# Two gated expert networks on one core: banks, silu buffers and background pieces dealt anew

## What is computed

```python
# first expert network: E=8 experts, hidden 256, two experts kept for each token
w = top2_softmax(xf @ Wg + bg)
for e in range(E):
    h = gelu(xf @ W1[e] + b1[e])
    out += w[:, e:e+1] * (h @ W2[e] + b2[e])
# windowed attention over the last 16 tokens
g = sigmoid(tanh(x @ Wp.T + bp) @ Wg.T)
out = windowed_sum(g * x, 16) / windowed_sum(g, 16)
# second expert network: E=16 experts, hidden 128, two kept
hidden = silu(x @ w1[e]) * (x @ w2[e])
out += dispatch[:, e] * (hidden @ w3[e])
# each of the three reads a layer-normalised t and adds to it: t = t + stage(ln(t))
```

## Time and profile before

| | us |
|---|---|
| median of 3 runs | 502.32 (501.47 to 503.74) |
| the profiled execution | 500.19 |
| its span, first to last instruction | 498.2 |
| first network, about | 284 to 372 |
| second network, about | 372 to 498 |

### The profile page before, as it was taken

The page is one execution under the profiler, slowest core; times in us unless marked ns, Lnnn a source line. Parts: engine busy times, 40 slices in busy tenths (PEclk is TensorE's granted clock), DMA queues, the critical chain, the costliest instruction groups (busy, mean ns, idle before and its releaser), DMA issues.

```text
span 498.2 us, 8873 instructions
## 1 busy us (share of the span) xinstructions
PE 442.7 (89%) x2982; PEld 299.8 (60%) x2982; DVE 352.8 (71%) x1029; ACT 278.7 (56%) x667; POOL 156.2 (31%) x189
## 2 busy tenths in 40 slices
PE   2998999959978999899999989998888888979994
PEld 2687777734537899799999834443434444534452
DVE  3288779338875768788969754655567999777863
ACT  1477666632307898788889666655564244333431
POOL 4400000001230748185204332323251453433342
PEclk9999999988988999999999999998999999999998
DMA  8200000000030033000000022111011122131230
GB/s 192 121 2 1 2 1 0 1 1 1 0 84 1 3 85 87 1 1 3 1 2 1 2 87 87 47 62 43 22 67 64 44 88 64 36 108 62 72 117 16
DMA packets 13324, 20.91 MB, mean 42 GB/s; under 512 B 4480, under 2 KB 6144, under 8 KB 12768
## 3 DMA queue, kind: packets, MB, share of 16 engines
q1 hardware_dynamic: 13136, 20.25, 14.2%
q10 hardware_dynamic: 144, 0.11, 0.1%
HBM read 19.62 MB, written 0.72 MB: 41 GB/s over the span
## 4 chain that ended last, share of the span: by engine, by line
PE 54%; DVE 29%; issue 7%; ACT 5%; POOL 2%; DMA 1%; DVEq 0%; POOLq 0%; SPq 0%; ACTq 0%
PE PS L1771 9%; PE PS L1515 7%; PE PS L1531 6%; PE PS L1782 5%; PE PS L1695 4%; PE PS L1707 3%; DVE stage L1393 3%; PE PS L1793 2%; DVE M L1039 2%; PE PS L1476 2%; PE PS L1607 2%; DVE pr L1284 2%; PE PS L1620 2%; ACT score_arena L776 2%; PE PS L1723 2%
## 5 line engine op out<-in xcount | busy, mean ns | idle before, releaser
L1771 PE MATMUL PS<-YTs,WH 64*128 64x512 f32 x192 | 80.3, 438 | 5.8 <-DVE stage L1393 3.1
L573 POOL TENSOR_TENSOR pr<-pr 128x512 f32<-128x512 f32 x39 | 50.3, 1291 | 97.3 <-DVE pr L1284 65.0
L1771 PE MATMUL PS<-YX,WH 64*128 64x512 f32 x192 | 80.5, 438 | 0.0
L776 ACT ACTIVATE score_arena<-score_arena,nmx 128x128 f32<-128x128 f32 (+1 forms) x128 | 56.9, 447 | 13.9 <-DVE nmx L1236 13.3
L849 ACT ACTIVATE VV<-PS 128x512 f32<-128x512 f32 x64 | 35.2, 594 | 41.5 <-PE PS L1771 41.5
L1771 PEld LDWEIGHTS PS<-YTs,WH 64*128 64x128 f32 x192 | 35.8, 186 | 34.0 <-ACT VV L849 9.1
L1393 DVE TENSOR_TENSOR stage<-VV,PS 128x512 f32<-128x512 f32 x64 | 41.2, 682 | 16.6 <-ACT VV L849 8.9
L831 ACT ACTIVATE stage<-PS,wk 128x512 f32<-128x512 f32 x64 | 40.5, 684 | 17.9 <-PE PS L1771 17.7
L717 ACT ACTIVATE st_mem<-PS 128x512 f32<-128x512 f32 x72 | 36.5, 615 | 21.6 <-PE PS L1531 21.6
L992 DVE TENSOR_TENSOR prod<-hats 128x768 f32<-128x768 f32 x48 | 42.5, 952 | 0.1
L1771 PEld LDWEIGHTS PS<-YX,WH 64*128 64x128 f32 x192 | 35.8, 186 | 4.3
(11 more groups left out here) (232 smaller groups left out, 1095.0 us busy)
## 6 DMA issues: line engine op xcount, KB each, us to landing
QH<-gate_store SPq DMA_DIRECT2D x96, 128.0 KB, 2.9
stage<-in_wexp SPq DMA_DIRECT2D x6, 512.0 KB, 6.0
wk<-in_w SPq DMA_DIRECT2D x1, 1034.0 KB, 8.0
wa<-in_wat SPq DMA_DIRECT2D x1, 768.0 KB, 6.2
cst<-in_consts SPq DMA_DIRECT2D x1, 611.0 KB, 6.4
X<-in_x SPq DMA_DIRECT2D x2, 256.0 KB, 5.1
out<-X SPq DMA_DIRECT2D x16, 32.0 KB, 1.9
wc<-in_w SPq DMA_DIRECT2D x2, 183.5 KB, 5.9
```

Source lines behind the costliest of these rows:

```text
L573: nc.gpsimd.tensor_tensor(acc[:, c % 2], acc[:, c % 2], weighted[:, u % 2], ALU.add).then_inc(acc_added, 1)
L776: ins = nc.scalar.activation(PR[:, s % 3, cols], MS[:, s % 3, cols], ACT.Exp, bias=nmx[:, s % 3, qt:qt + 1], scale=-1.0, accum_out=rsum[:, ...
L1771: ins = mm(PS[:, banks[i], :], w[hs, m, tiles[i] * P:(tiles[i] + 1) * P], ys[i][hs, cs], start=(k == 0), stop=(k == 2))
```

## The change

The second network's V products take three banks in turn (1, 6, 5), its silus read banks 0 and 2, and the outputs of both networks take two banks (3, 4). Silu results have four buffers. The waits follow: V of r waits for the first product of r-1 alone, silu n for product n-4, an output for the combine of two units before. Further, pieces move to other slots on all engines, and DVE pieces of the second network can now stand between the two products (`i == 0`) or between the second product and the combine (`i == 1`). Its core:

```diff
-OUT_BANKS = (3, 4, 5)
+OUT_BANKS = (3, 4)
+SILU_BANKS = (0, 2)
+V_BANKS = (1, 6, 5)
-        sil = VV[:, 0]
+        sil = VV[:].rearrange("p a b n -> p (a b) n")
...
-                if n >= 2:
-                    act.wait_ge(prod3_done, n - 1)
-                nc.scalar.activation(sil[:, n % 2], PS[:, HID_BANKS[2 * n % 4], :], ACT.Silu).then_inc(silu_done, 1)
+                if n >= 4:
+                    act.wait_ge(prod3_done, n - 3)
+                nc.scalar.activation(sil[:, n % 4], PS[:, SILU_BANKS[n % 2], :], ACT.Silu).then_inc(silu_done, 1)
...
-                    nc.vector.tensor_tensor(hid[:, n % 4], sil[:, n % 2], PS[:, HID_BANKS[(2 * n + 1) % 4], :], ALU.mult).then_inc(prod3_done, 1)
+                    nc.vector.tensor_tensor(hid[:, n % 4], sil[:, n % 4], PS[:, V_BANKS[n % 3], :], ALU.mult).then_inc(prod3_done, 1)
...
-                if ht == 0 and u >= 3:
-                    pe.wait_ge(combined, u - 2)
+                if ht == 0 and u >= 2:
+                    pe.wait_ge(combined, u - 1)
...
-                        pe.wait_ge(prod3_done, 2 * r)
+                        pe.wait_ge(prod3_done, 2 * r - 1)
```

More of the change, by code:

```diff
@@ L834, in _ @@
                     y_evac("zB", 2)
[L835 to L840, removed]
@@ L841, in _ @@
-                if n in (29, 49):
-                    tanh({29: 0, 49: 1}[n])
+                if n == 3:
+                    copy_rows("tB", 0)
+                if n == 9:
+                    copy_rows("tB", 1)
+                    y_high(3, True)
+                    copy_rows("tB", 2)
+                if n == 11:
+                    y_evac("yB", 3)
+                if n == 17:
+                    y_evac("zB", 3)
+                if n == 25:
+                    y_high(0, False)
+                if n == 27:
+                    y_evac("yC", 0)
@@ new lines, in _ @@
+                if n == 31:
+                    copy_rows("tB", 3)
+                if n == 33:
+                    tanh(0)
+                if n == 42:
+                    y_high(0, True)
+                if n == 43:
+                    y_evac("yD", 0)
+                if n == 45:
+                    y_high(1, False)
+                if n == 47:
+                    y_evac("yC", 1)
+                if n == 49:
+                    tanh(1)
+                if n == 51:
+                    y_evac("zD", 0)
@@ L845, in _ @@
+                if n == 60:
+                    copy_rows("tD", 0)
+                if n == 62:
+                    y_high(1, True)
+                if n == 63:
+                    y_evac("yD", 1)
             for n in range(4 * E3):
                 act.wait_ge(hid3_ready, n // 2 * 2 + 1)
-                if n >= 2:
-                    act.wait_ge(prod3_done, n - 1)
-                nc.scalar.activation(sil[:, n % 2], PS[:, HID_BANKS[2 * n % 4], :], ACT.Silu).then_inc(silu_done, 1)
-                if n in (1, 15, 20, 36):
-                    y_high(*{1: (2, False), 15: (2, True), 20: (3, False), 36: (3, True)}[n])
@@ new lines, in _ @@
+                nc.scalar.activation(sil[:, n % 4], PS[:, SILU_BANKS[n % 2], :], ACT.Silu).then_inc(silu_done, 1)
+                if n == 2:
+                    y_high(2, False)
+                if n == 3:
+                    y_evac("yC", 2)
+                if n == 6:
+                    tanh(2)
+                if n == 7:
+                    y_evac("zD", 1)
+                if n == 13:
+                    copy_rows("tD", 1)
+                if n == 17:
+                    y_high(2, True)
+                    y_evac("yD", 2)
@@ new lines, in _ @@
+                if n == 20:
+                    y_high(3, False)
+                if n == 21:
+                    y_evac("zD", 2)
+                if n == 23:
+                    y_evac("yC", 3)
+                if n == 26:
+                    tanh(3)
+                if n == 27:
+                    copy_rows("tD", 2)
+                if n == 29:
+                    output(0)
+                if n == 36:
+                    y_high(3, True)
+                if n == 39:
+                    y_evac("yD", 3)
@@ L860, in _ @@
+                if n == 43:
+                    y_evac("zD", 3)
+                if n == 45:
+                    output(1)
+                if n == 47:
+                    copy_rows("tD", 3)
+                if n == 58:
+                    output(2)
             output(3)
@@ L1378, in _ @@
                     window_add(1)
-                    ln_stats(1)
+                    ln_center(1)
+                    ln_variance(1)
                 if u == 14:
-                    ln_stats(2)
+                    ln_center(2)
+                    ln_variance(2)
                     ln_low(1)
@@ L1403, in _ @@
                 if r == 3:
-                    window_logits(2)
                     top_second(E3)
-                if r == 4:
-                    take_sum("fC", 3)
-                    window_gate(2)
-                    top_gate(1, E3)
-                if r == 5:
-                    window_add(2)
-                    ln_center(2)
                 if r == 6:
```

121 lines of the change are left out of this document (66 added, 55 removed), and 5 rows, old and new, of tables (FIRST_FILLS, SECOND_FILLS).

## The result

The changed kernel takes 493.15 us in the median of 4 runs (491.05 to 494.26), the kernel before 501.89 in the runs beside it; ratio 0.9844, 95% interval 0.9808 to 0.9880, so 6.0 to 9.6 us faster. The forecast was 495.3, in a range of 490.5 to 500.0.

A forecast was written before the change was run, and what follows sets the result against it. TensorE, busy 89% of the span, was taken as the bound, with DVE bounding 389 to 425 us. Terms 4.6 + 0.4 + 4.2 - 0.1 - 1.05 - 1.0 = 7.0 us off 502.3 gave 495.3 us, range 490.5 to 500.0.

The forecast's parts named there:

- First network: All moves up to the fill yD 1, waits and one clock fall together: gain 4.7, rounded down to 4.6 us.
- tB 2 with yB 3: First network's start: two key fills share slot 5, gelus unblocked from y_high of chunk 3; gain 0.3 us.
- yD 0: First-network key fill waiting 2.08 us for ln_low(0): wait falls to about 0.7, gain 1.4, plus 1.7 of clock.
- Slots 0 to 13: Second network from yD 1 to fE 0: old waits go, new holds come, idle 10.1 to 9.7; gain 0.4 us.
- Slots 14 to 19: Second network, fE 0 to yD 3: earlier ln_variance(3) cuts the 2.56 us wait to 0.6; gain 4.2, 1.7 clock.
- Slots 20 to 31: Second network's end: three fills in one slot wait twice, loss 0.1 us; output(2) between silus 58 and 59, loss 1.05.
- rival B: Waits in slots 10 and 11 and at yD 1 make the clock fall again: 498.7 us, chance 0.12.
- S 30: Split pass of slot 30, waiting for ACT because output(2) stands between silus 58 and 59; loss 1.05 us.
- Short waits: Second network: about 2 us of idle in waits under 0.1 us, half expected to stay; loss 1.0 us.
- A: DVE bounds 389 to 425 us, so removed stretches by POOL's adds pay in full, 2.8 us: 492.9, chance 0.21.
- C: The waits only move and the clock falls twice, so almost nothing is gained: about 501 us, chance 0.08.
- D: Slower: DVE pieces between the products hold outputs in slots 5 and 8 to 12; 506.7 us, chance 0.06.

The follow-up runs named there:

- slots alone: The changed kernel with the old banks and buffers, so only the new slots; 497.0 us, ratio 0.9936 to the kernel before.
- banks alone: The kernel before with only the change's banks, buffers and waits, all pieces in their old slots; 502.51 us, ratio 1.0017.
- short adds: POOL's 39 adds cut from 512 columns to 8, in the changed kernel (488.07 us) and in the kernel before (492.16 us).
- both repairs: The changed kernel with output(2) back behind silu 59 and slots 20 to 22 as before; 492.08 us, ratio 0.9810 to the kernel before.

## Why the prediction was right

- **First network, 4.6 forecast, 5.2 measured.** tB 2 with yB 3 gave its 0.2 to 0.3 us; yD 0 waits 0.75 (0.7 forecast); the clock's fall was priced 1.7 and measures 1.5 to 1.6. yC 1 waits 0.18 where I had 0.6, and the last wait is 1.10 where I had 1.5: these two make most of the difference.
- **Slots 0 to 13, 0.4 forecast, 0.1 measured.** The new holds eat what the stretches give, wait by wait: 1.41 at the output of slot 10 (1.8), 1.06 at yC 3 (0.6), 0.86 at yD 2 (0.9), 0.67 at zD 2 (0.6), 1.10 at wC 2 (1.1), 0.69 at pC 2 (0.8). But the count that these waits stood in was wrong. I put TensorE's work at 46.2 us and its idle time at 10.1, falling to 9.7. The stretches from yD 1 to fE 0, before and after:

```profile
370.30:426.55 56.25, 48.45 (x295) 24.58 (x295) 47.98 (x111) 22.99 (x42) 22.59 (x21) 1.00 0.22 68
...
365.02:421.19 56.17, 47.13 (x294) 25.28 (x295) 43.88 (x110) 22.88 (x42) 22.62 (x21) 1.00 0.22 75
```

The idle time was 7.8 us and rose to 9.0, and busy time fell by 1.3 with the same matmuls at the same clock, which I had not foreseen and no run explains. That the two nearly cancel, and the part came out near my 0.4, is luck.
- **Slots 14 to 19, 4.2 forecast, 4.3 measured.** The fall there is 1.5 of it. It is the places that do it: the slots alone keep it (19.14 us), the banks alone don't (21.75 without a fall), and short adds in the old order leave a wait of 3.12 at S 19. Which of the moved pieces it is was not tested.
- **Slots 20 to 31.** Forecast was a loss of 0.1 up to tD 3; measured 1.4. The waits were right (0.78 and 0.60), the fall behind them I had only in rival B and at another place. S 30 lost 1.04 (1.05 forecast).
- **Short waits.** I had read some 2 us of TensorE's idle time in the second network as waits under 0.1 us. There are none: the 12.5 us of idle between 372 and 488 us all stand in waits of 0.1 us and more, and what I missed was busy time. The loss of 1.0 that I added from it had no ground and did not come. Without it and with the fall at slot 22 the sum would have been 7.0 + 1.0 - 1.3 = 6.7; the parts measure 5.2 + 0.1 + 4.3 - 1.4 - 1.0 = 7.2. So it is partly luck that 7.0 came so close: two terms were wrong by 1 us or more in opposite ways. The time of 495.3 was 2.2 us too long all the same: the medians differ by 8.7 us, the two profiled executions by 6.8 (500.19 to 493.35) and their parts by 7.2. What the medians have beyond the parts lies in the spread between executions.
- **The rivals.** A (stretches in full): not for the change, whose part up to fE 0 is unchanged. Its mechanism is real, though: short adds give the old order 4.4 us there, and brought fE 0 of the new one 2.5 us forward. B (the clock falls again): half of it, in the changed kernel's profile at slot 22, and in that of the kernel with both repairs, which is the same code up to there, at slot 11. A fall in slots 10 to 12 was on my list of signs of being wrong. C and D did not come. D's hold in slot 10 was there (3.5 us from the first product at 406.24 us to the second at 409.76, where it is 0.6 without pieces) and cost 1.41, but putting the pieces back saved nothing, so it only took the place of another wait.
- **The ports.** By the rule of the Trainium skill (SBUF — State Buffer, Who interferes with whom) alone the second network was to gain some 5.7 us. From yD 1 to tD 3, one fall in each, it gained 94.68 - 91.65 = 3.0. I had 8 of 14 stretches going; 9 went, and their sum fell from 10.1 to 3.1 us. Short adds take out all 14, and take 94.68 - 88.82 = 5.9 us off the old order there. So the rule tells which instructions stretch; what a us of stretch is worth on the path is, by an estimate from these sums, some 0.4 to 0.6 us. The products stay at 682 ns on average, as before.

## What to carry to other kernels

When background work is interleaved by hand, list the fills that a bottleneck engine waits for and price each move by when the next of them can start: that came within 0.6 us in four of five parts here, in one of them by luck; the fifth was off by 1.3 us for a fall of the clock, which such a list does not tell. Take the idle time from the busy time of the stretch, not from a pace times a count: mine was 2.3 us too high that way. Before dealing pieces anew, ask what stretches them: the adds on POOL beside two-input DVE work cost the old order 9.2 us, and the new deal won back 5.6, so a cheaper add could be worth more than a better place. (The runs with short adds leave most of the sum out, so 9.2 us is the most that it could give.) A third buffer pays only with an order that uses it (nothing measurable alone, 2.3 us with the new slots, by the parts of one execution).

## What the runs showed of the hardware

- **A fall of the clock is not fixed by the wait before it.** It fell behind waits of 1.41 and 1.06 us in slots 10 and 11 in one of five profiles, behind 0.78 and 0.60 in slot 22 in five of seven, and behind the 2.56 to 3.15 us at S 19 in four of five: of two profiles with 3.15 us there, one has the fall and one has not. It costs 1.5 to 1.6 us each time (one in the kernel with the slots alone lasted three times as long). Falls ahead of 284 us also come and go: tB 0 starts between 288.6 and 291.4 us in these profiles. Together they make up much of the spread between runs of one kernel: over 29 runs of the kernel before, the clock's loss (1 less the mean granted clock, times the span) goes from 7.0 to 14.5 us, and the longer times have the larger loss (correlation 0.89).
- **A power on POOL did not stretch DVE.** POOL and DVE of the changed kernel, timeline, at the same time:

```profile
380.35 1.02 POOL L549 TENSOR_TENSOR tg<-cst,tg 128x4 f32<-128x4 f32 x1 [1.32 <-DVE tg L1367]
```

```profile
380.78 0.21 DVE L1244 SCALAR_TENSOR_TENSOR tg<-tg 128x64 f32<-128x64 f32 x1
381.03 0.22 DVE L1226 TENSOR_REDUCE tg<-tg 128x4 f32<-128x64 f32 x1
381.29 0.23 DVE L1228 TENSOR_TENSOR tg<-tg 128x64 f32<-128x64 f32 x1
```

L1244 and L1228 have two SBUF inputs and run at their usual time inside POOL's 1.02 us on 4 elements. In these fourteen profiles 45 such DVE instructions start inside a power, 0.28 us or more behind its start, and none takes over 0.02 us more than its shortest; none happens to start earlier than that. Beside an add of 512 elements they took up to 1.48 us (L1109 of the kernel before, at 317.43 us, 0.41 elsewhere). How long an instruction lasts on POOL does not tell how much it holds up DVE.
